# Attention logits from 64-row f32 products in two row halves, and the next pair's projection between the two transposes of a slot

## The chip, the cores and the metric

One NeuronCore of a Trainium2 chip runs the whole kernel. The metric is the time of one execution on the device in microseconds. The kernel before takes 1675.25 us, the median of 3 runs (1672.22 to 1677.1). The profiled execution took 1675.05 us, of which 1673.3 us are the span of the trace.

## What is computed

The input X is 32 sequences of 256 rows of 128 values, all f32. The output is X plus an attention plus a mixture of eight experts, both fed with the layer norm of X:

```python
x = L0_attn_X                       # (32, 256, 128)
xn = _layernorm(x)
x = x + attn(xn) + ffn(xn)

# attention: H = 16 heads of DQ = 64, NB = 10
Q, K, V = xn @ Wq + bq, xn @ Wk, xn @ Wv        # each (32, 16, 256, 64)
R = xn @ Wr + br                                 # (32, 16, 256, 10)
extra = einsum('bhtn,ntp->bhtp', R, D_ntT)       # bias by distance t - p, window of 128
logits = einsum('bhtd,bhpd->bhtp', Q, K) / 8 + bias + extra    # bias masks p > t and t - p >= 128
A = softmax(logits) @ V                          # (32, 256, 16 * 64)
return A @ Wproj + bproj

# ffn: of 8 experts (gelu, 512 wide) the two with the largest router logit
```

Rows 0 to 127 of a sequence see keys 0 to 127; rows 128 to 255 see all 256 keys. A head therefore has 3 x 128 columns of logits for 128 partitions.

## The kernel before, in words

Five engines run their own instruction lists and meet at semaphores: PE (TensorE), DVE (VectorE), ACT (ScalarE), POOL (GpSimd), and SP, which issues the DMAs. The kernel has four stages: a preparation up to about 150 us (loads, layer norm, router, weights), the attention of sequences 0 to 15, the experts (754 to 1004 us), and the attention of sequences 16 to 31. In each half POOL moves rows for the experts beside the attention, and in the second half DVE also adds the experts' rows to the output (`add_rows`, L1165, lines L1176).

Each half runs its first sequence, then a loop with two sequences in its body and seven turns, then its last sequence. The order of the work is written out by hand: `sequence` exists once for each engine and runs over 8 slots; slot j belongs to head pair j (heads 2j and 2j+1) of the sequence. There is no planner. An engine waits at a semaphore in the order in which its own code stands, so everything behind a waiting instruction waits too.

The logits of a pair are not computed from Q and K. Preparation makes one 128x128 matrix per head, `wm` (Wk of the head times Wq of the head, centred and scaled; L1278), split into an fp32r high part and an fp32r low part. `keys` (L1419) multiplies it with the transposed rows `xq`, also split, in three fp32r products for each head (`product`, L1331 to L1336). ACT rounds the result out of PSUM to `key_hi` (L810), and DVE subtracts that from the same PSUM bank to make `key_lo` (L1093). `logits` (L1437) then multiplies `xq` and the keys, again in three products: three of 256 columns for query rows 0 to 127 of both heads and three of 512 columns for rows 128 to 255.

One slot j of PE before:

1. `keys` of pair j+1 (6 products, 256 columns each)
2. `turn_probs` of head 2(j-3)+1: three 128x128 transposes (L1433)
3. `logits` of pair j (6 products)
4. the slot's unit at place 0
5. in even slots the values product of four heads (L1475; f32, 64 output columns in two column halves of the array, 8 products in 16 records), in odd slots the output product of four heads (L1487; 4 products in 8 records)
6. `turn_probs` of head 2(j-2)
7. the slot's unit at place 1

A unit is a piece of other work for this or the next sequence, always through one PSUM bank (`MISC_BANK`): "v" (V projection, 3 products of 512 columns), "r" (R projection, 6 products of 256 columns), or "g" (distance bias, one product of 512 columns, L1404). The table is UNITS at L358: 4 v, 2 r and 8 g per sequence.

DVE in slot j before: reciprocal of the sums of pair j-1 (L1121), copy of the transposed probabilities (`copy_probs`, L1111), `key_lo` of pair j+1, the four additions of logits and `extra` with their row minima (L1137, two of 128 columns, then two of 256), a second `copy_probs`, and copies of g units with tile 0 (L1088). ACT before: `key_hi` of pair j+1, its unit copies (v L784, r L790, g with tile 1 L795), the four exponentials of pair j (L826), and in even slots `headT` (L835). POOL scales the probabilities of pair j-1 (L687, L689), rounds the r unit of the slot before (L662) and issues the row moves.

PSUM has 8 banks. Before: keys 1, logits 3, transposes 1, values 1, units 1, outputs 1. The output product of a sequence accumulates over its four quads in one bank, and DVE adds it to `acc` once per sequence (L1160).

Of the kernel before, what the change touches and what calls it, by code (L numbers as in the profile page):

```python
# [5 lines left out]
ALU = mybir.AluOpType  # L6
# [7 lines left out]
P = 128  # L14
BANK = 512
# [33 lines left out]
def build(nc, X, Wq, bq, Wk, Wv, Wproj, bproj, Wr, br, b_nd, router_w, w1, b1, w2, b2, out):  # L49
# [24 lines left out]
    with ctx:  # L74
# [17 lines left out]
        wm_hi = sb("wm_hi", [P, H, P], F32R)  # L92
        wm_lo = sb("wm_lo", [P, H, P], F32R)
# [59 lines left out]
        wq_r = sb("wq_r", [P, H * DQ])  # L153
        wk_r = sb("wk_r", [P, H * DQ])

        top[0] = shared
        wqT = sb("wqT", [P, PAIRS, P])
        wkT = sb("wkT", [P, PAIRS, P])
# [14 lines left out]
        bq_r = sb("bq_r", [PAIRS, P])  # L173
        bqT = sb("bqT", [P, PAIRS])
        br_bc = sb("br_bc", [P, H * NB])
        qsum = sb("qsum", [P, PAIRS])
        ksum = sb("ksum", [P, PAIRS])
# [21 lines left out]
        key_hi = sb("key_hi", [P, 2, 2, T], F32R)  # L199
        key_lo = sb("key_lo", [P, 2, 2, T], F32R)  # L200
# [39 lines left out]
        def skew_rows(tile, head, count, first, size, pitch):  # L240
# [63 lines left out]
        key_high = sem("key_high")  # L304
        key_low = sem("key_low")
        s0_psum = sem("s0_psum")
        logit0_made = sem("logit0_made")
        s1_psum = sem("s1_psum")
        g_act = sem("g_act")
        g_dve = sem("g_dve")  # L310
        mean_psum = sem("mean_psum")
        centred = sem("centred")
        wq_centred = sem("wq_centred")
# [22 lines left out]
        PREP = [("w2", NX, False), ("small", 4, False), ("wq", 2, False), ("wk", 2, False),  # L336
                ("brev", 1, False), ("wm", 4, True), ("w1", NX, True)]
# [13 lines left out]
        H_BANK, Y_BANK, XB_BANK = (0, 1, 2, 3), (4, 5), (6, 7)  # L351
        KEY_BANK, S1_BANK, S0_BANK, PT_BANK, HEAD_BANK, MISC_BANK, OUT_BANK = 0, (1, 2), 3, 4, 5, 6, 7
        WR_MEAN_BANK, WV_MEAN_BANK = 5, (6, 7)
# [4 lines left out]
        UNITS = [(0, 0, "g", 2, 1, 0), (1, 0, "r", 0, 0, 1), (1, 1, "g", 3, 0, 0), (2, 0, "g", 3, 1, 0),  # L358
# [3 lines left out]
        UNITS_FINAL = [unit for unit in UNITS if not unit[5]]  # L362
        START = [("r", 0, 0), ("r", 1, 0), ("g", 0, 0), ("g", 0, 1), ("g", 1, 0), ("g", 1, 1), ("v", 0, 0), ("g", 2, 0)]
# [14 lines left out]
        def unit_taken(engine, kind, k, t, seq):  # L378
# [6 lines left out]
            elif t == 1:  # L385
                engine.wait_ge(g_act, 4 * seq + (k + 1))
            else:
                engine.wait_ge(g_dve, 4 * seq + (k + 1))
# [1162 lines left out]
```

## Time and profile before

| | value |
|---|---|
| median of 3 runs | 1675.25 us |
| profiled execution | 1675.05 us, span 1673.3 us |
| PE busy | 1510.8 us, 90% |
| PE weight loads busy | 1276.9 us, 76% |
| DVE busy | 1066.7 us, 64% |
| ACT busy | 988.9 us, 59% |
| POOL busy | 804.1 us, 48% |
| share of PE in the chain that ended last | 72% |

PE records overlap, because a product starts while the one before it drains; a duration of one record is longer than its distance to the next. How long PE takes for a piece of work is read from the start of its first record to the start of the next piece. A line of the timeline merges equal records and shows their count as x16, and the idle time before it, if any, in brackets with what ended it. A row of the windows view gives, for a stretch, its length and then the busy time of PE, weight loads, DVE, ACT and POOL, the granted clock of TensorE, and the DMA share.

### The profile page before, as it was taken

The numbers are of one execution on the slowest core, as the hardware profiler recorded it, in microseconds if no ns is written. First come the engines' busy times: TensorE is split into PE (matmuls) and PEld (weight loads), VectorE is DVE, ScalarE is ACT, GpSimd is POOL, SyncE is SP. The second block draws the span as 40 slices with busy tenths as digits, with TensorE's granted clock in tenths as the row PEclk, the third lists the DMA queues.
The fourth block names the chain that finished last, engine by engine and source line by source line (L and its number), as shares of the span: only waits on it lengthen the run. The fifth ranks groups of instructions, "written<-read, shape, count | busy, mean of one in ns | idle before, by whom it ended". The sixth has DMA issues, their size and how long they took to land.

```text
span 1673.3 us, 42585 instructions
## 1 busy us (share of the span) xinstructions
PE 1510.8 (90%) x10864; PEld 1276.9 (76%) x10864; DVE 1066.7 (64%) x3749; ACT 988.9 (59%) x2999; POOL 804.1 (48%) x1515
## 2 busy tenths in 40 slices
PE   2555999999999999989999997998989898989997
PEld 2224887878878887878999996787878787877885
DVE  5585777777767777762211112787868786877775
ACT  2223776766766676755554443676757675766664
POOL 0322766666666666650000001665656565656654
PEclk8686999999999999999999998999999999999999
DMA  9774555655555555655666664565555555656552
GB/s 285 271 274 120 163 168 145 177 166 165 155 160 168 152 159 145 180 154 160 201 202 205 206 202 136 155 174 135 167 143 161 150 149 143 166 142 180 145 158 70
DMA packets 375709, 282.62 MB, mean 169 GB/s; under 512 B 16626, under 2 KB 349988, under 8 KB 375588
## 3 DMA queue, kind: packets, MB, share of 16 engines
q1 hardware_dynamic: 367396, 264.64, 53.9%
q0 software_dynamic: 8192, 16.79, 3.5%
q14 instruction: 97, 0.79, 0.2%
q8 instruction: 24, 0.39, 0.1%
HBM read 168.05 MB, written 113.26 MB: 168 GB/s over the span
## 4 chain that ended last, share of the span: by engine, by line
PE 72%; DVE 9%; issue 8%; ACT 4%; SPq 3%; DMA 2%; DVEq 1%; POOL 1%; ACTq 0%; POOLq 0%
PE ps L1336 11%; PE ps L1334 11%; PE ps L1335 11%; PE ps L1475 10%; PE ps L1433 10%; PE ps L1370 8%; PE ps L1487 6%; PE ps L1404 3%; ACT prob L826 2%; DVE logit L1137 2%; DVE gst L1088 1%; DVE probT L1111 1%; DVE acc L1176 1%; SPq L453 1%; PE ps L1352 1%
## 5 line engine op out<-in xcount | busy, mean ns | idle before, releaser
L826 ACT ACTIVATE prob<-logit,low 128x128 f32<-128x128 f32 (+1 forms) x1024 | 454.2, 446 | 149.4 <-DVE low L1137 123.3
L1111 DVE COPY probT<-ps 128x384 f32<-128x384 f32 x512 | 284.5, 556 | 204.5 <-PE ps L1433 192.6
L687 POOL TENSOR_SCALAR prob<-prob,inv 128x128 f32<-128x128 f32 x512 | 188.6, 368 | 346.3 <-DVE inv L1121 336.7
L1137 DVE CUSTOM_DVE_ANT_0 logit<-ps,extra 128x128 f32<-128x128 f32 (+1 forms) x1024 | 303.3, 353 | 0.7 <-PE ps L1336 0.4
L1433 PE MATMUL ps<-ident,prob 128*128 128x128 f32 x1536 | 264.0, 281 | 12.1 <-DVE probT L1111 7.3
L1475 PE MATMUL ps<-probT,val 128*64 128x256 f32 (+1 forms) x2048 | 203.1, 342 | 44.1 <-DVE probT L1111 42.7
L689 POOL TENSOR_SCALAR prob<-prob,inv 128x256 f32<-128x256 f32 x512 | 241.4, 472 | 0.0
L1475 PEld LDWEIGHTS ps<-probT,val 128*64 128x64 f32 x2048 | 131.8, 141 | 130.7 <-issue 82.6
L1433 PEld LDWEIGHTS ps<-ident,prob 128*128 128x128 f32 x1536 | 175.0, 142 | 48.2 <-issue 40.7
L1334 PE MATMUL ps<-key_hi,xq_hi 128*128 128x256 f32 (+1 forms) x512 | 194.9, 381 | 0.0
L826 ACT ACTIVATION_READ_ACCUMULATOR prob<-logit,low 128x1 f32 x1024 | 192.9, 188 | 0.0
L662 POOL CAST r_hi<-r_raw 120x512 fp32r<-120x512 f32 x64 | 39.1, 610 | 301.7 <-ACT r_raw L790 301.7
L1093 DVE TENSOR_TENSOR key_lo<-ps,key_hi 128x512 fp32r<-128x512 f32 x256 | 175.3, 685 | 12.5 <-ACT key_hi L810 8.3
L1335 PE MATMUL ps<-key_lo,xq_hi 128*128 128x256 f32 (+1 forms) x512 | 175.2, 342 | 0.0
L1336 PE MATMUL ps<-key_hi,xq_lo 128*128 128x256 f32 (+1 forms) x512 | 174.0, 340 | 0.0
L810 ACT CAST key_hi<-ps 128x512 fp32r<-128x512 f32 x256 | 148.1, 579 | 34.3 <-PE ps L1336 34.3
L1334 PE MATMUL ps<-xq_hi,wm_hi 128*128 128x256 f32 x512 | 153.2, 299 | 4.5 <-DVE key_lo L1093 4.5
L672 POOL DMA_INDIRECT x_place<-xrow,at_now x128 | 131.9, 1031 | 39.9 <-issue 25.3
L1192 DVE TENSOR_TENSOR yrow<-ps,w2b 128x512 f32<-128x512 f32 x39 | 27.0, 692 | 189.7 <-PE ps L1370 189.7
L1370 PEld LDWEIGHTS ps<-w2b,hid 128*128 128x128 f32 x1248 | 145.2, 192 | 3.3
L674 POOL DMA_INDIRECT yget<-y_place,at_now x128 | 130.4, 1018 | 35.9 <-issue 24.3
L1335 PE MATMUL ps<-xq_lo,wm_hi 128*128 128x256 f32 x512 | 146.8, 287 | 0.0
(188 smaller groups left out, 3088.2 us busy)
## 6 DMA issues: line engine op xcount, KB each, us to landing
skew<-gst SPq DMA_DIRECT2D x256, 256.0 KB
extra<-skew SPq DMA_DIRECT2D x128, 512.0 KB, 3.9
extra<-skew SPq DMA_DIRECT2D x128, 256.0 KB, 3.6
w1b<-w_d SPq DMA_DIRECT2D x39, 514.0 KB, 3.5
w2b<-w_d SPq DMA_DIRECT2D x39, 320.0 KB, 3.3
x_place<-zero SPq DMA_DIRECT2D x39, 256.0 KB, 2.7
placed<-x_place SPq DMA_DIRECT2D x39, 256.0 KB, 3.7
y_place<-yrow SPq DMA_DIRECT2D x39, 256.0 KB, 2.2
```

What stands on the lines that cost most here:

```text
L687: nc.gpsimd.tensor_scalar(prob[:, h, 0:P], prob[:, h, 0:P], inv[:, h, 0:1], 1.0, ALU.mult, ALU.mult).then_inc(norm_made, 1)
L689: nc.gpsimd.tensor_scalar(prob[:, h, P:], prob[:, h, P:], inv[:, h, 1:2], 1.0, ALU.mult, ALU.mult).then_inc(norm_made, 1)
L826: ins = nc.scalar.activation(prob[:, h % PB, a:b], logit[:, h % LB, a:b], ACT.Exp, scale=-1.0, bias=low[:, h % LB, t:t + 1], accum_out=tot ...
L1093: nc.vector.tensor_tensor(key_lo[:, pair % 2, :, :].rearrange("p n k -> p (n k)"), ps[:, KEY_BANK, :], key_hi[:, pair % 2, :, :].rearrange ...
L1111: nc.vector.tensor_copy(probT[:, h % 4, :], ps[:, PT_BANK, 0:3 * P]).then_inc(pT_made, 1)
L1137: ins = nc.vector.tensor_tensor_reduce(out=logit[:, h % LB, a:b], in0=src, in1=extra[:, h, a:b], scale=1.0, scalar=BIG, op0=ALU.add, op1=A ...
L1334: nc.tensor.matmul(dst, a_hi, b_hi, start=start, stop=False)
L1335: nc.tensor.matmul(dst, a_hi, b_lo, start=False, stop=False)
L1336: return nc.tensor.matmul(dst, a_lo, b_hi, start=False, stop=stop)
L1370: mm = nc.tensor.matmul(ps[:, Y_BANK[u], t * P:(t + 1) * P], hid[:, u, c, t * P:(t + 1) * P], w2b[:, u, c * P:(c + 1) * P], start=(c == 0) ...
L1433: mm = nc.tensor.transpose(ps[:, PT_BANK, n * P:(n + 1) * P], prob[:, h % PB, n * P:(n + 1) * P], ident[:, :])
L1475: mm = nc.tensor.matmul(ps[DQ * n:DQ * n + DQ, HEAD_BANK, q], val[:, s, v:v + DQ], probT[:, hh % 4, p], start=(s == 0), stop=(s == 1), ski ...
```

## The change

`wm` is gone. The weights stay separate: `wqk`, centred Wq plus bias and centred Wk with the scale, each [128, 1024], split into high and low parts in preparation. `keys` of a pair now makes Q and K of both heads: for w in (Wq, Wk), three fp32r products of 256 columns. One ACT copy takes the bank to `qk`, in f32 and unsplit; DVE does nothing to it. `logits` of a pair is four f32 products with a contraction of 64: head 2j in rows 0 to 63 of the array, head 2j+1 in rows 64 to 127, each with its own PSUM bank. DVE's four additions wait for all of them.

The order in a slot changes on every engine. PE: logits of pair j; values or outputs; transposes of head 2(j-2); unit at place 0; keys of pair j+1; transposes of head 2(j-2)+1; unit at place 1. ACT: exponentials of pair j, then the unit copy (v or r), then the copy of pair j+1, then `headT`. DVE: reciprocal, four additions, `add_heads` in odd slots, both `copy_probs`, the g copy (all g copies are now DVE's), then the r correction of the same slot (L1102, before in the slot after). POOL rounds the r unit in its own slot too, ahead of the row moves.

The output product has no bank of its own any more. It goes into the bank of the values product, and DVE adds it to `acc` after each quad, four times per sequence instead of once.

```diff
-        UNITS = [(0, 0, "g", 2, 1, 0), (1, 0, "r", 0, 0, 1), (1, 1, "g", 3, 0, 0), (2, 0, "g", 3, 1, 0),
-                 (3, 0, "v", 0, 1, 0), (3, 1, "v", 1, 0, 0), (4, 0, "g", 0, 0, 1), (4, 1, "g", 0, 1, 1),
-                 (5, 0, "v", 1, 1, 0), (5, 1, "r", 1, 0, 1), (6, 0, "g", 1, 0, 1), (6, 1, "g", 1, 1, 1),
-                 (7, 0, "v", 0, 0, 1), (7, 1, "g", 2, 0, 1)]
+        UNITS = [(0, 0, "v", 0, 0, 0), (0, 1, "g", 3, 0, 0), (1, 0, "r", 0, 0, 1), (1, 1, "g", 3, 1, 0),
+                 (2, 0, "v", 0, 1, 0), (2, 1, "g", 0, 0, 1), (3, 0, "v", 1, 0, 0), (3, 1, "g", 0, 1, 1),
+                 (4, 0, "r", 1, 0, 1), (4, 1, "g", 1, 0, 1), (5, 0, "v", 1, 1, 0), (5, 1, "g", 1, 1, 1),
+                 (6, 1, "g", 2, 0, 1), (7, 1, "g", 2, 1, 1)]
...
 # PE
-                wait_from(pe, key_low, i * PAIRS + pair)
-                for n in range(2):
-                    h = 2 * pair + n
-                    mm = product(ps[:, KEY_BANK, n * T:n * T + T],
-                                 ((wm_hi[:, h, :], wm_lo[:, h, :]), (xq_hi[:, par, :], xq_lo[:, par, :])))
+                wait_from(pe, key_made, i * PAIRS + pair)
+                cols = slice(pair * P, (pair + 1) * P)
+                for w in range(2):
+                    mm = product(ps[:, KEY_BANK, w * T:(w + 1) * T],
+                                 ((wqk_hi[:, w, cols], wqk_lo[:, w, cols]), (xq_hi[:, par, :], xq_lo[:, par, :])))
...
+            def logits(i, pair):
+
+                pe.wait_ge(key_made, i * PAIRS + pair + 1)
                 wait_from(pe, logit_made, i * PAIRS + pair - 1)
-                product(ps[:, S1_BANK[pair % 2], :].rearrange("p (n k) -> p n k", n=2),
-                        ((xq_hi[:, par, P:T], xq_lo[:, par, P:T]),
-                         (key_hi[:, pair % 2, :, :], key_lo[:, pair % 2, :, :]))).then_inc(s1_psum, 1)
+                for q, k, cols in ((slice(0, P), slice(0, P), slice(0, P)), (slice(P, T), slice(0, T), slice(P, 3 * P))):
+                    for n in range(2):
+                        rows = slice(DQ * n, DQ * n + DQ)
+                        mm = nc.tensor.matmul(ps[:, S_BANK[pair % 2][n], cols], qk[rows, pair % 2, 0, q],
+                                              qk[rows, pair % 2, 1, k], start=True, stop=True)
+                mm.then_inc(s_psum, 1)
...
             def sequence(i, par, start, heads=True, more=True):
                 for j in range(PAIRS if heads else LAG):
+                    if heads:
+                        logits(i, j)
+                    if j % 2 == 0 and here(i, j - 4, heads, start):
+                        values(i, (j - 4) // 2)
+                    if j % 2 == 1 and here(i, j - 5, heads, start):
+                        outputs(i, (j - 5) // 2)
+                    if here(i, j - 2, heads, start):
+                        turn_probs(i, 2 * (j - 2))
+                    if heads:
+                        units(i, par, j, 0, more)
                     if heads and (j + 1 < PAIRS or more):
                         keys(i if j + 1 < PAIRS else i + 1, par if j + 1 < PAIRS else 1 - par, (j + 1) % PAIRS)
-                    if here(i, j - 3, heads, start):
-                        turn_probs(i, 2 * (j - 3) + 1)
...
                     if here(i, j - 2, heads, start):
-                        turn_probs(i, 2 * (j - 2))
+                        turn_probs(i, 2 * (j - 2) + 1)
                     if heads:
                         units(i, par, j, 1, more)
...
 # ACT, in sequence: the copy of the next pair behind the exponentials
-                    if heads and (j + 1 < PAIRS or more):
-                        keys(i if j + 1 < PAIRS else i + 1, (j + 1) % PAIRS)
-                    for n, kind, k, t, ahead in units_at(j, 0, more) if heads else []:
-                        unit(len(START) + i * len(UNITS) + n, kind, k, t, i + ahead)
...
                         ins.then_inc(prob_made, 1)
+                    for n, kind, k, t, ahead in units_at(j, 0, more) if heads else []:
+                        unit(len(START) + i * len(UNITS) + n, kind, k, t, i + ahead)
+                    if heads and (j + 1 < PAIRS or more):
+                        keys(i if j + 1 < PAIRS else i + 1, (j + 1) % PAIRS)
...
 # DVE
-                nc.vector.tensor_tensor(key_lo[:, pair % 2, :, :].rearrange("p n k -> p (n k)"), ps[:, KEY_BANK, :],
-                                        key_hi[:, pair % 2, :, :].rearrange("p n k -> p (n k)").bitcast(F32),
-                                        ALU.subtract).then_inc(key_low, 1)
...
+                        wait_apart(dve, s_psum, i * PAIRS + j + 1, const_made)
...
+            def add_heads(i, quad):
+                dve.wait_ge(out_psum, i * QUADS + (quad + 1))
+                wait_from(dve, attn_added, i * QUADS + quad)
+                seq = i if quad >= 0 else i - 1
+                x = acc[:, at(2 * seq, 2), :]
+                nc.vector.tensor_tensor(x, ps[:, HEAD_BANK, 0:2 * E].rearrange("p (t e) -> p t e", t=2), x,
+                                        ALU.add).then_inc(attn_added, 1)
...
 # preparation: transposes of Wq and Wk and the products to wm are gone; bq is loaded to all partitions
-            sp.dma_start(bq_r[:, :], bq.rearrange("(k d) -> k d", d=P)).then_inc(small_in, 16)
+            sp.dma_start(bq_bc[:, :], bq.partition_broadcast(P)).then_inc(small_in, 16)
```

## Rows read from the trace of the kernel before

**Rows 1.** Windows: one clean sequence, then the seven turns, of either half.

```profile
187.90:224.00 36.10, 35.95 (x275) 30.61 (x274) 27.81 (x104) 25.52 (x87) 24.23 (x47) 1.00 0.58 166
187.90:710.50 522.60, 507.81 (x3812) 431.65 (x3810) 389.67 (x1443) 360.99 (x1205) 338.58 (x643) 0.99 0.56 162
...
1111.70:1148.30 36.60, 36.13 (x275) 30.60 (x273) 29.75 (x112) 25.92 (x87) 24.15 (x47) 1.00 0.60 167
1075.00:1623.10 548.10, 516.16 (x3812) 436.37 (x3809) 416.13 (x1555) 364.04 (x1205) 337.57 (x643) 0.98 0.56 155
```

**Rows 2.** Timeline of PE: start us, length us, what (count).

```profile
504.62 0.48 PE L1334 MATMUL ps<-wv_hi,xq_hi 128*128 128x512 f32 x1
...
505.40 0.28 PE L1334 MATMUL ps<-xq_hi,wm_hi 128*128 128x256 f32 x1
...
505.99 0.28 PE L1336 MATMUL ps<-xq_hi,wm_lo 128*128 128x256 f32 x1
506.11 0.49 PE L1433 MATMUL ps<-ident,prob 128*128 128x128 f32 x3
506.35 0.37 PE L1334 MATMUL ps<-key_hi,xq_hi 128*128 128x256 f32 x1
...
507.48 0.39 PE L1404 MATMUL ps<-basis,rT 120*128 120x512 f32 x1
507.80 1.52 PE L1475 MATMUL ps<-probT,val 128*64 128x256 f32 x16
509.25 0.55 PE L1433 MATMUL ps<-ident,prob 128*128 128x128 f32 x3
509.64 0.50 PE L1404 MATMUL ps<-basis,rT 120*128 120x512 f32 x1
...
512.79 1.05 PE L1487 MATMUL ps<-wproj,headT 128*128 128x128 f32 x8
513.68 0.49 PE L1433 MATMUL ps<-ident,prob 128*128 128x128 f32 x3
```

**Rows 3.** Timeline of DVE, same columns, the bracket is idle time before.

```profile
507.79 0.28 DVE L1137 CUSTOM_DVE_ANT_0 logit<-ps,extra 128x128 f32<-128x128 f32 x1
...
508.90 0.69 DVE L1088 COPY gst<-ps 128x512 f32<-128x512 f32 x1
...
514.21 0.56 DVE L1111 COPY probT<-ps 128x384 f32<-128x384 f32 x1 [0.68 <-PE ps L1433]
...
519.65 0.74 DVE L1102 SCALAR_TENSOR_TENSOR rT<-r_hi,minus_low,r_raw 120x512 fp32r<-120x512 f32 x1
```

**Rows 4.** Groups by line, DVE, 1100 to 1640 us: count, busy us, mean ns.

```profile
L1176 DVE SCALAR_TENSOR_TENSOR acc<-yget,wtop,acc 128x128 f32 (+1 forms) x112 | 31.9, 347 | 0.0
```

**Rows 5.** Timeline of ACT, same columns.

```profile
508.41 0.40 ACT L826 ACTIVATE prob<-logit,low 128x128 f32<-128x128 f32 x1 [1.35 <-DVE low L1137]
...
510.18 0.56 ACT L835 COPY headT<-ps 128x512 f32<-128x512 f32 x1
...
515.24 0.57 ACT L790 COPY r_raw<-ps 120x512 f32<-120x512 f32 x1
515.70 0.58 ACT L810 CAST key_hi<-ps 128x512 fp32r<-128x512 f32 x1
```

**Rows 6.** Timeline around START: an ACT copy, and PE that waited for it.

```profile
145.75 0.58 ACT L795 COPY gst<-ps 128x512 f32<-128x512 f32 x1 [3.75 <-DMA skew<-gst]
...
146.38 0.79 PE L1334 MATMUL ps<-wv_hi,xq_hi 128*128 128x512 f32 x1 [1.83 <-ACT gst L795]
```

**Rows 7.** Timeline of DVE and PE at a turn of the loops.

```profile
487.33 0.18 DVE L1121 RECIPROCAL inv<-total 128x4 f32<-128x4 f32 x1 [2.81 <-issue]
...
488.33 2.83 PE L1475 MATMUL ps<-probT,val 128*64 128x256 f32 x16 [2.43 <-DVE probT L1111]
...
1311.60 0.18 DVE L1121 RECIPROCAL inv<-total 128x4 f32<-128x4 f32 x1 [4.12 <-issue]
```

**Rows 8.** The only 64-row product of the program, in preparation (length min/median/max).

```profile
L1278 PE MATMUL ps<-wqT,wkT x32: 272/272/419, 42.4 to 45.5; 64*128 64x128 f32 x32
```

More of the change, by code:

```diff
@@ L690, in sequence @@
                                                     ALU.mult, ALU.mult).then_inc(norm_made, 1)
-                    for n, kind, k, t, ahead in units_at(j - 1, 0, more) + units_at(j - 1, 1, more):
-                        if kind == "r" and heads:
+                    for n, kind, k, t, ahead in units_at(j, 0, more) if heads else []:
+                        if kind == "r":
                             round_weights(i + 1, k)
@@ L829, in sequence @@
                         ins.then_inc(prob_made, 1)
+                    for n, kind, k, t, ahead in units_at(j, 0, more) if heads else []:
+                        unit(len(START) + i * len(UNITS) + n, kind, k, t, i + ahead)
+                    if heads and (j + 1 < PAIRS or more):
+                        keys(i if j + 1 < PAIRS else i + 1, (j + 1) % PAIRS)
                     if j % 2 == 0 and here(i, j - 4, heads, start):
@@ L836, in sequence @@
                                        ps[:, HEAD_BANK, :]).then_inc(head_made, 1)
-                    for n, kind, k, t, ahead in units_at(j, 1, more) if heads else []:
-                        unit(len(START) + i * len(UNITS) + n, kind, k, t, i + ahead)
             def experts(b, u, k):
@@ L1121, in sequence @@
                         nc.vector.reciprocal(inv[:, h:h + 2, :], total[:, h:h + 2, :]).then_inc(inv_made, 1)
-                    if here(i, j - 3, heads, start):
-                        copy_probs(i, 2 * (j - 3) + 1)
-                    if heads and (j + 1 < PAIRS or more):
-                        keys(i if j + 1 < PAIRS else i + 1, (j + 1) % PAIRS)
                     if heads:
@@ L1207, in _ @@
                 for n, (kind, g, t) in enumerate(START):
-                    if kind == "g" and t == 0:
+                    if kind == "g":
                         positions(s0 * len(UNITS) + n, s0, g, t)
-                keys(s0, 0)
                 sequence(s0, s0)
@@ new lines, in values @@
+            def values(i, quad):
+                h = 4 * quad + 3
+                if quad == 0:
+                    pe.wait_ge(val_made, 4 * i + 2)
+                if quad == -2:
+                    pe.wait_ge(val_made, 4 * i)
+                pe.wait_ge(pT_made, i * H + h + 1)
+                wait_from(pe, attn_added, i * QUADS + quad)
+                for pair in range(2):
+                    for s in range(2):
+                        q = slice(pair * T, (pair + 1) * T) if s == 0 else slice(pair * T + P, (pair + 1) * T)
+                        p = slice(0, T) if s == 0 else slice(T, 3 * P)
+                        for n in range(2):
+                            hh = h - 3 + 2 * pair + n
+                            v = hh % H * DQ
+                            mm = nc.tensor.matmul(ps[DQ * n:DQ * n + DQ, HEAD_BANK, q],
+                                                  val[:, s, v:v + DQ], probT[:, hh % 4, p],
+                                                  start=(s == 0), stop=(s == 1), skip_group_check=True)
+                mm.then_inc(head_psum, 1)
@@ new lines, in outputs @@
+            def outputs(i, quad):
+                pe.wait_ge(head_made, i * QUADS + (quad + 1))
+                for t in range(2):
+                    for pair in range(2):
+                        mm = nc.tensor.matmul(ps[:, HEAD_BANK, t * E:(t + 1) * E],
+                                              headT[:, pair, t * P:(t + 1) * P],
+                                              wproj[:, (2 * quad + pair) % PAIRS, :],
+                                              start=(pair == 0), stop=(pair == 1))
+                mm.then_inc(out_psum, 1)
```

229 lines of the change are left out of this document (71 added, 158 removed).

## The prediction

> **What bounds the kernel now.** I read the windows first. In a clean sequence of the first half PE is busy 35.95 of 36.10 us, in the second half 36.13 of 36.60 us, at a granted clock of 1.00; DVE has 28 to 30 us and ACT 26 us of work in it [rows 1]. So PE sets the pace, and a slot is 4.5 us of PE work. Seven turns of the loop are fourteen sequences: 14 x 36.10 = 505.4 of 522.60 us, and 14 x 36.60 = 512.4 of 548.10 us [rows 1]. The rest, 17.2 and 35.7 us, together 52.9 us, falls on the six jumps back in each half: DVE stands idle there for 2.81 us (4.12 us in the second half) with nothing to wait for, and PE then waits for its `copy_probs` [rows 7].
>
> Next the timeline of PE, for the price of each piece, as the distance from its start to the next piece [rows 2]: v behind transposes 0.78; keys 0.71; three transposes 0.24, behind the values product 0.39; logits 1.13 (506.35 to 507.48); g 0.32 ahead of the values, where the array changes its tiling (a product of 512 columns without that is 0.23, so the change is 0.09); values 1.45; outputs 0.89.
>
> **The new logits on PE.** The values product is the nearest row: f32, pairs of products in the two column halves. 16 records are 8 pairs, four of 256 and four of 128 columns, in 1.45 us. The new logits are 8 records, two pairs of each kind: 0.73 us. With one change of tiling behind them, 0.82 us in place of 1.13. That takes the row halves to run side by side as the column halves do; the only 64-row product there is stands in one half at a time and does not tell [rows 8]. Bounds: 0.73, if the changes are in the 1.45 already; 1.54, if the halves do not overlap at all. In between: the weight loads of 128 columns might go one behind the other. Outputs have 8 such records in 0.89 us [rows 2], so that gives 0.98.
>
> The trace shows 0.09 us at a change of tiling, ahead of the values. The Trainium skill, TensorEngine Tiling (Array Packing), Key Properties, says that a change of tiling mode drains the array, while tiles of one mode load weights and multiply in parallel. The first half speaks against the change, with two more switches in every slot, 256 x 0.18 = 46 us by the row's price; the second half supports the 0.73.
>
> Keys keep their six products of 256 columns, transposes, values, outputs and the units keep their number. So PE's own work falls by 0.31 us per slot less the entry into the logits (0.09).
>
> **What ends last in a slot now: two chains.** Before, ACT and DVE had made the split keys of pair j+1 before they touched the logits of pair j. Now PE makes pair j+1 late in slot j, ACT copies it behind the exponentials of pair j, and the next thing PE does after T1 and one g is the logits that wait for it. Behind that wait stand all values, outputs and transposes. I count from the first record of logits j.
>
> Chain A, over PE. Even slot with a unit: logits 0.82, values 1.45, transposes 0.39, v (or r) 0.78, keys 0.71: issued by 4.15. The last record begins 0.12 before that and lasts 0.28 [rows 2]; the next engine starts 0.04 later (transposes end at 514.17, DVE starts at 514.21 [rows 2, 3]); the copy takes 0.58 [rows 5]; PE goes on 0.05 after an ACT copy (146.33 to 146.38 [rows 6]). Sum: 4.98. PE has only T1 and g to put beside it, 4.15 + 0.24 + 0.32 = 4.71: it waits 0.27. Slot 6, without v (and 0.08 for the step out of the transposes): 4.28. Odd slot: 0.82 + 0.89 + 0.24 + 0.78 + 0.71 = 3.44, so 4.27; slot 7: 3.57.
>
> Chain B, over DVE and ACT. The last pair of the logits begins at 0.51 and lasts 0.39, as a record of 512 columns does (an f32 product passes its 256 columns more than once) [rows 2]: 0.90. DVE starts 0.04 later, plus 0.12 for its second wait with a register (an estimate between 0 and 0.25, no row): 1.06. The exponentials begin 0.62 after the first addition (507.79 to 508.41 [rows 3, 5]) and take 1.77 (508.41 to 510.18 [rows 5]): 3.45. The unit copy 0.46 (515.24 to 515.70), the copy 0.58, PE 0.05: 4.54. In slots 6 and 7 no unit copy stands there: 4.08.
>
> Each slot takes the later: 0, 2 and 4 take 4.98 (A), 6 takes 4.28 (A), 1, 3 and 5 take 4.54 (B), 7 takes 4.08 (B). Sum 36.92.
>
> **DVE work that comes in the way.** It lost `key_lo` and got all g copies (0.69), four `add_heads` and, in slots 1 and 4, the r correction (0.74 [rows 3]) at the end of the same slot. In slot 4 the second transposes end at 4.64; `copy_probs`, g, r and the reciprocal, one behind the other, last until 6.5, and the additions of slot 5 were due at 4.98 + 1.06 = 6.04. So slot 5 is 0.48 longer. In slots 2 and 3 chain A covers the same or there is no r. Sum 37.40, against 36.10: +1.30 per sequence, x 16 = +21 us.
>
> In the second half `add_rows` adds four operations of 31.9/112 = 0.28 us, 1.14 us, at the end of slots 1 and 2 [rows 4]. Slot 1: g waits for the r copy (4.02), is out at 4.50; g copy, r, add_rows and reciprocal last until 7.02; due was 5.60. 1.42 late: slot 2 takes 4.54 + 1.42 = 5.96, 0.98 more than by A. Slot 2 ends in the same way 0.76 late, which slot 3 pays. 37.40 + 1.74 = 39.14, against 36.60: +2.54, x 16 = +41 us.
>
> **The jumps back.** DVE's last work in slot 7 is the g copy, which ends at 4.18. With the same pause of 2.81 us its additions start at 7.2 and not at 5.14: 2.05 late, slot 0 takes 6.59 for 4.98, +1.6. Second half, 1.31 more: +2.9. Six of each: 27 us against 52.9: -26 us. PE no longer waits for `copy_probs` there, and the slack of the other slots is gone anyway. DVE's list for the loop gets a few instructions shorter, so the pause might vanish (a rival below).
>
> The rows show DVE idle at the jump, released by nothing. The Trainium skill, Runtime: NRT & Kernel Launch, Instruction fetch mechanics, says that a taken branch to a target outside the small window of loaded instructions forces a fetch before the engine goes on; the trace agrees. Only a list that fits the window would be spared.
>
> **At nothing.** The output product's own bank: DVE's additions sit between slots and the next values follow 2 us later; without that cover 0.4 us per quad, 50 us. SP's writes and reads of the distance bias keep their number, and their g units come at least two slots ahead of the additions that need them. POOL's r rounding now waits for ACT in its own slot and holds up a row move of 1 us; POOL has 24 of 36 us of work [rows 1]. Preparation loses transposes and copies and gains a load of half a megabyte: between -3 and +3 us, I take 0. Experts: unchanged.
>
> **Sum.** +21 + 41 - 26 = +36 on the profiled execution's 1675.05 us, which is the median of the runs within 0.2 us: 1710 us in round numbers.
>
> **Rivals.**
>
> 1. *The chains are shorter than their sum, and PE sets the pace again.* For it: PE alone would need 33.4 + 8 x 0.09 = 34.2 us per sequence; every link was taken from rows where the engine was not hurried. Against it: the links stand in one line by the code, and each is a measured length. Full effect: 16 x (34.2 - 36.1) + 16 x (34.2 - 36.6) - 26 = -95, 1580 us. A chain shorter by 0.1 us per slot is 26 us; from 0.14 us per slot it decides for faster; at 0.27 (no wait in even slots) it is 1640 us. Chance 0.25.
> 2. *The halves load their weights one behind the other.* +0.16 us per slot, 256 slots, +41: 1751 us. Chance 0.12.
> 3. *The row halves do not overlap.* 1.54 for 0.82: +184: 1895 us. Chance 0.06. The pairs of the values product speak against it; nothing in the trace excludes it.
> 4. *DVE's loop fits now and the pause goes.* 27 us less: 1683 us, about no change. For it: fewer instructions in the body. Against: the body loses `key_lo` and one set of waits per slot but gets g copies and `add_heads`, a few per cent in all. Chance 0.07.
>
> My forecast has 0.50, with an own range of 1690 to 1735 (0.1 us per slot either way). Faster by over 0.3% (5 us, about what a measurement of this kernel can tell from none): most of rival 1 and a little of the forecast's edge, 0.27. Slower: forecast, 2, 3 and part of 4, 0.67. Between: 0.06. The range 1635 to 1775 leaves out rival 3, the full form of rival 1 and little else.
>
> **What would show it.** PE idle in every slot just ahead of the logits, released by the ACT copy, 0.2 to 0.3 us in even and 0.5 in odd slots; a busy PE of about 33 us in a sequence of 37.4 and 39.1 us; logits records in pairs, 0.73 us from first record to the next piece; longer slots 5, and 2 and 3 in the second half, with DVE still at r or `add_rows` when the logits are there. Sequences under 36 us would make it wrong in sign. Records of the logits one after another would be rivals 2 or 3. Equal sequences before and after with shorter jumps would be rival 4 or a part of 1.

## The result, and the profile after

The changed kernel takes 1731.24 us, the median of 4 runs (1727.19 to 1740.91), beside 1675.99 us of the kernel before on the same chip: ratio 1.034, 95% interval 1.030 to 1.039. It is slower by 55 us. The forecast was 1710 us, 35 us slower.

The page of the profile first, the lines that say most:

```profile
span 1730.2 us, 43010 instructions
PE 1533.4 (89%) x11335; PEld 1185.5 (69%) x11335; DVE 1024.0 (59%) x3715; ACT 924.8 (53%) x2864; POOL 807.1 (47%) x1515
PE 59%; ACT 14%; issue 10%; DVE 9%; SPq 4%; DVEq 1%; DMA 1%; POOL 1%; ACTq 0%; POOLq 0%
L1351 PE MATMUL ps<-basis,rT 120*128 120x512 f32 x256 | 129.4, 506 | 56.6 <-ACT val L757 36.3
L1391 PEld LDWEIGHTS ps<-qk 64*128 64x128 f32 x2048 | 137.3, 190 | 88.7 <-ACT qk L776 69.9
```

The third line is the chain that ended last: ScalarE has come into it. The last two lines show what PE now waits for: the unit copy (`val`) ahead of a g product, and the copy of the projection (`qk`) ahead of the logits, where the wait is booked on the weight load. Both copies stand behind the exponentials on ScalarE.

The windows of the changed kernel answer to [rows 1]: a clean sequence, then the seven turns, of the first and of the second half (window, its length, then busy us of PE, PE's weight loads, DVE, ACT and POOL, granted clock, DMA share, GB/s).

```profile
464.36:502.08 37.72, 36.35 (x288) 27.84 (x289) 26.21 (x103) 23.97 (x82) 24.49 (x47) 1.00 0.56 163
190.51:738.99 548.48, 518.72 (x4033) 396.48 (x4033) 368.38 (x1429) 335.35 (x1148) 340.69 (x644) 0.98 0.54 155
1391.57:1431.20 39.63, 37.15 (x289) 27.86 (x289) 28.42 (x111) 23.97 (x82) 24.24 (x47) 1.00 0.54 152
1102.33:1678.84 576.51, 528.09 (x4032) 395.45 (x4033) 397.37 (x1541) 335.46 (x1148) 338.87 (x644) 0.99 0.53 147
```

Against [rows 1] the turns take 25.9 and 28.4 us more, 54.3 of the 56.9 us by which the span grew. Clean sequences: 14 x (37.72 - 36.10) + 14 x (39.63 - 36.60) = +65.1 us. Turns less 14 clean sequences: 20.4 + 21.7 = 42.1 us, where it was 52.9: -10.8 us. The first logits start at 152.4 us, where they started at 153.6, so preparation, put at nothing, is 1.2 us shorter.

Distances between the starts of successive logits, slots 0 to 7, from the trace (clean sequences):

```
forecast, half 1       4.98 4.54 4.98 4.54 4.98 5.02 4.28 4.08   37.40
after, half 1          4.93 4.56 4.94 4.56 4.96 4.97 4.28 4.51   37.71
forecast, half 2       4.98 4.54 5.96 5.30 4.98 5.02 4.28 4.08   39.14
after, half 2          4.95 4.56 5.92 5.37 4.96 5.14 4.28 4.46   39.64
```

One odd slot (slot 1) of the changed kernel, in the timeline of PE, DVE and ACT, answers to [rows 2, 3, 5]:

```profile
469.29 0.93 PE L1391 MATMUL ps<-qk 64*128 64x128 f32 x8
470.15 1.16 PE L1421 MATMUL ps<-wproj,headT 128*128 128x128 f32 x8
...
470.36 0.29 DVE L1093 CUSTOM_DVE_ANT_0 logit<-ps,extra 128x128 f32<-128x128 f32 x1
...
470.99 0.40 ACT L788 ACTIVATE prob<-logit,low 128x128 f32<-128x128 f32 x1 [1.26 <-DVE low L1093]
...
472.76 0.56 ACT L763 COPY r_raw<-ps 120x512 f32<-120x512 f32 x1
472.90 0.49 PE L1380 MATMUL ps<-ident,prob 128*128 128x128 f32 x3
473.22 0.58 ACT L776 COPY qk<-ps 128x512 f32<-128x512 f32 x1
...
473.38 0.49 PE L1351 MATMUL ps<-basis,rT 120*128 120x512 f32 x1
473.85 0.93 PE L1391 MATMUL ps<-qk 64*128 64x128 f32 x8
```

That is the forecast's chain B link by link: additions 1.07 after the logits' start (1.06 forecast), exponentials 0.63 later (0.62), 1.77 for them, 0.46 for the unit copy, 0.63 for the copy and the step to PE. The logits take 0.86 (469.29 to 470.15; 0.82 forecast).

### The profile page after: what moved, and what is told of

Same layout as the page of the kernel before. It is cut to its first block, busy times and chain, and to the rows that moved or that the text cites. A ratio compares the mean times of both kernels' runs of the same rounds, so it can differ in the third digit from the quotient of the medians.

```text
span 1730.2 us, 43010 instructions
## 1 busy us (share of the span) xinstructions
PE 1533.4 (89%) x11335; PEld 1185.5 (69%) x11335; DVE 1024.0 (59%) x3715; ACT 924.8 (53%) x2864; POOL 807.1 (47%) x1515
## 4 chain that ended last, share of the span: by engine, by line
PE 59%; ACT 14%; issue 10%; DVE 9%; SPq 4%; DVEq 1%; DMA 1%; POOL 1%; ACTq 0%; POOLq 0%
PE ps L1391 11%; ACT prob L788 9%; PE ps L1316 8%; PE ps L1411 8%; PE ps L1380 6%; PE ps L1280 5%; PE ps L1282 5%; PE ps L1281 5%; PE ps L1351 4%; PE ps L1421 4%; DVE logit L1093 2%; ACT val L757 2%; ACT qk L776 2%; DVE acc L1135 1%; DVE rT L1064 1%
## 5 line engine op out<-in xcount | busy, mean ns | idle before, releaser
L1391 PE MATMUL ps<-qk 64*128 64x128 f32 (+1 forms) x2048 | 243.0, 356 | 14.5 <-ACT qk L776 8.0
L1057 DVE COPY gst<-ps 128x512 f32<-128x512 f32 x256 | 175.7, 686 | 58.3 <-PE ps L1351 48.4
L1391 PEld LDWEIGHTS ps<-qk 64*128 64x128 f32 x2048 | 137.3, 190 | 88.7 <-ACT qk L776 69.9
L1411 PE MATMUL ps<-probT,val 128*64 128x256 f32 (+1 forms) x2048 | 194.7, 332 | 2.7 <-issue 1.4
L1411 PEld LDWEIGHTS ps<-probT,val 128*64 128x64 f32 x2048 | 127.1, 136 | 81.5 <-issue 43.0
L1351 PE MATMUL ps<-basis,rT 120*128 120x512 f32 x256 | 129.4, 506 | 56.6 <-ACT val L757 36.3
L776 ACT COPY qk<-ps 128x512 f32<-128x512 f32 x256 | 148.3, 579 | 37.0 <-PE ps L1282 30.2
L1421 PEld LDWEIGHTS ps<-wproj,headT 128*128 128x128 f32 x1024 | 129.4, 198 | 44.9 <-issue 43.1
L1421 PE MATMUL ps<-wproj,headT 128*128 128x128 f32 x1024 | 154.2, 296 | 1.4 <-ACT headT L801 1.4
L1280 PE MATMUL ps<-xq_hi,wqk_hi 128*128 128x256 f32 x512 | 151.4, 296 | 0.0
```

The source lines that it names most:

```text
L1280: nc.tensor.matmul(dst, a_hi, b_hi, start=start, stop=False)
L1351: mm = nc.tensor.matmul(ps[:, MISC_BANK, :], rT[:, n // 2, a:a + P], basis[:, :], start=True, stop=True)
L1391: mm = nc.tensor.matmul(ps[:, S_BANK[pair % 2][n], cols], qk[rows, pair % 2, 0, q], qk[rows, pair % 2, 1, k], start=True, stop=True)
L1411: mm = nc.tensor.matmul(ps[DQ * n:DQ * n + DQ, HEAD_BANK, q], val[:, s, v:v + DQ], probT[:, hh % 4, p], start=(s == 0), stop=(s == 1), ski ...
L1421: mm = nc.tensor.matmul(ps[:, HEAD_BANK, t * E:(t + 1) * E], headT[:, pair, t * P:(t + 1) * P], wproj[:, (2 * quad + pair) % PAIRS, :], st ...
```

## The experiments

All times are medians with the ratio to the kernel before, measured beside it on the same chip. "After" stands at 1.034.

| run | us | ratio (interval) |
|---|---|---|
| old order, 64-row logits | 1629.1 | 0.974 (0.971 to 0.977) |
| projection right behind the logits | 1823.9 | 1.090 (1.087 to 1.094) |
| after, DVE loops written out | 1673.2 | 1.001 (0.999 to 1.002) |
| logits head by head | 1729.1 | 1.034 (1.031 to 1.037) |
| one more exponential on ACT | 1811.3 | 1.082 (1.080 to 1.084) |
| projection of Q twice on PE | 1769.8 | 1.056 (1.054 to 1.058) |
| both heads in one row half | 1850.6 | 1.105 (1.102 to 1.107) |
| old order, DVE loops written out | 1608.5 | 0.960 (0.959 to 0.962) |
| before, DVE loops written out | 1620.0 | 0.969 (0.966 to 0.972) |
| projection alone put back | 1830.7 | 1.094 (1.091 to 1.098) |
| old order, transposes together | 1839.8 | 1.101 (1.098 to 1.104) |
| old order, projection of Q twice | 1699.3 | 1.017 (1.013 to 1.021) |

**The arithmetic with the old order.** PE, ACT and DVE get the order of before. The products stay those of the change, and so do the new table of units, DVE's copies of g and the bank that values and outputs share.

```diff
 PE, slot j:
+    keys(j + 1)
+    turn_probs(i, 2 * (j - 3) + 1)
     logits(i, j)
+    units(place 0)
     values or outputs
     turn_probs(i, 2 * (j - 2))
-    units(place 0)
-    keys(j + 1)
-    turn_probs(i, 2 * (j - 2) + 1)
     units(place 1)
 ACT, slot j:
+    keys(j + 1); units(place 0)
     exponentials(j)
-    units(place 0); keys(j + 1)
 DVE: copy_probs(2(j-3)+1) to the slot's head, r correction one slot later
```

> The changed kernel's arithmetic (64-row float32 logits, both projections), with the order of the kernel before on PE, ACT and DVE: projection of the next pair at the slot's head, its copy ahead of the exps, one transpose at the head and one at the end, r correction and second probability copy a slot later. Theory (the copy of the projection behind the exps makes the two chains): both chains are gone, PE sets the pace with 34.2 us a sequence worked out from its pieces against 37.7 and 39.7 measured in the changed kernel, so about 1731 - 16 x 3.5 - 16 x 5 = 1595, up to 1625 if half 2 keeps its add_rows waits. Rival (the new logits themselves, or PE's own work, make it slow, and the order is innocent): 1700 or more.

Measured 1629.1 us, 43 us faster than before and 102 us faster than after. That is 4 us above the top of the expected range, but the chain theory held and the rival fell. The order costs 1.034 - 0.974 = 6.05%, 101 us. All the rest of the change gains 2.6%, 44 us: the new arithmetic, together with the table of units and the shared bank, which no run separates from it. The windows (clean sequences of the two halves) show PE busy throughout:

```profile
446.75:482.22 35.47, 35.47 (x290) 27.85 (x289) 26.75 (x103) 23.80 (x83) 24.24 (x47) 1.00 0.59 169
1321.04:1356.69 35.65, 35.65 (x290) 27.90 (x289) 28.50 (x111) 23.73 (x83) 24.46 (x47) 1.00 0.63 175
```

35.5 us, not the 34.2 that I had taken from PE's pieces. An even slot is 4.95 with nothing waited for. The transposes ahead of the logits take 0.42 to 0.48 to the logits' start, where three transposes took 0.24:

```profile
460.58 0.49 PE L1381 MATMUL ps<-ident,prob 128*128 128x128 f32 x3
461.00 0.93 PE L1392 MATMUL ps<-qk 64*128 64x128 f32 x8
```

Behind the logits, v up to the values takes 0.90 where v up to the projection takes 0.78, but 0.08 of that is the step into the values, which the forecast had priced; its first product takes 0.34 behind the logits and 0.32 behind transposes. Outputs right behind the logits take 0.99 for 0.89 (470.15 to 471.14 in the changed kernel).

**One more operation on ScalarE, one more on PE.** The two chains predict different prices for added work.

```diff
+ nc.scalar.activation(spare[...], logit[head 2j+1, long part], ACT.Exp, ..., accum_out=spare[...])
```

> The changed kernel with one more ScalarE instruction pair in each slot, behind the four exps: the last long exponential once more, into a spare tile (0.49 us with its accumulator read in the changed kernel's trace). Nothing waits for it but what stands behind it on ScalarE, the copies. Theory (the copy behind the exps is in the chain of every slot): slots 1, 3, 5 and 7 take the whole 0.49, slots 0, 2, 4 and 6, where the copy starts 0.05 to 0.15 after ScalarE was free, 0.35 to 0.45: 3.4 to 3.7 us a sequence, 1731 + 108 to 120 = 1839 to 1851. Rival (PE sets the pace, ScalarE is 53% busy): 1731.

Measured +80 us, below the 108 to 120 expected. Slots 1, 3 and 5 take the whole of it (4.56 to 5.05 in slots 1 and 3), slots 0, 2, 6 and 7 take 0.2 to 0.4, slot 4 only 0.1: a sequence grows by 2.8, not by 3.5, and the jumps give another 12 us back. Every slot grows by added ScalarE work, but I had overrated by how much in the even ones. An engine busy 53% of the span decides here; the rival that PE sets the pace would have seen nothing. The waits of PE between 190 and 640 us (what PE waited for, us in total, times, longest), first after, then this run:

```profile
PE ps L1351 <- ACT val L757: 7.6, 16, 0.8
```

```profile
PE ps L1355 <- ACT val L758: 24.2, 42, 1.2
```

```diff
-                for w in range(2):
+                for w in (0, 0, 1):
                     mm = product(ps[:, KEY_BANK, ...
```

> The changed kernel with the Q half of each pair's projection computed twice (three more products of 256 columns, 0.355 us on PE in each of 256 slots, same result). Theory (two chains, PE's lateness binds slots 0, 2, 4 and 6 alone; in slots 1, 3 and 7 the projection ends about 0.6 us before ScalarE is free to copy it): 0.3 to 0.36 in four slots of eight, nothing in the others: 1731 + 38 to 46 = 1769 to 1777, and the odd slots stay at 4.56 and 4.4. Rival (PE sets the pace): 0.355 in each slot, 1731 + 91 = 1822. Rival (only ScalarE's chain): 1731.

Measured 1769.8 us, inside the expectation, though not in each slot as expected: slots 0, 2, 4 and 6 took 0.32 to 0.37, slots 1 and 3 rose from 4.56 to 4.80, and slot 7 fell to 4.24. My 0.6 of slack in odd slots was too much: in slot 1 after, the projection's last record ends at 473.06 and its copy starts at 473.22. The lines of such a slot in this run show why it took 4.80:

```profile
487.36 0.48 PE L1351 MATMUL ps<-basis,rT 120*128 120x512 f32 x1
487.96 0.93 PE L1391 MATMUL ps<-qk 64*128 64x128 f32 x8
```

PE still waits here, 0.60 from g's start to the logits for 0.32 of work, now for the copy of a late projection. That is chain A. Without the added 0.36 it is 4.44 long in an odd slot (the forecast had 4.27), only 0.12 under chain B. So the two chains stand close together in odd slots, and a third of the added PE work was covered. PE's own work is below both.

The same PE edit in the kernel with the old order:

> The kernel with the order of before and 64-row logits (1629 us), with the Q half of each projection computed twice, as in the run that cost the changed kernel 39 us. Theory (with this order PE sets the pace in every slot): 0.355 in each of 256 slots, 1629 + 91 = 1720, between 1710 and 1722. Rival (waits for VectorE or ScalarE set part of the slots here too): 1665 to 1690.

Measured 1699.3, +70 us. Slots 1 to 4 and 6 grew by 0.35 or 0.36 (4.95 to 5.31, 4.25 to 4.61), slot 7 by 0.32, slots 0 and 5 by 0.29 and 0.25: PE sets the pace there, but for some 0.1 us of slack in slots 0 and 5. A clean sequence grew by 2.64 and 2.47 us, 82 us in 32 of them; 12 us come back at the jumps, whose extra time fell from 30.5 to 18.8 us. I had let the jumps stay as they were, and so was 20 us too high.

**The row halves.** Only the order of the four products changes:

```diff
-  for q, k, cols in (short, long):
-      for n in range(2):
+  for n in range(2):
+      for q, k, cols in (short, long):
```

> The changed kernel with the four products of a pair's logits issued head by head (head 0 short and long, then head 1 short and long) instead of the two heads alternating. Theory (products in the two row halves overlap only with a neighbour in the other half): now only the long one of head 0 meets the short one of head 1, so logits take about 1.2 us instead of 0.86, 0.3 to 0.4 more in each of 256 slots: 1731 + 75 to 100 = 1805 to 1830. Rival (no overlap in either order): 1731 unchanged. Rival (the two run beside each other in any order): 1731 too, with logits at 0.86.

Measured: no change, 1729.1 us; logits 0.86. (Beneath the unchanged total a clean sequence was 0.26 and 0.43 us shorter in the two halves, in slot 7 and in slot 5 of the second half; the turns cost 6 us more beyond their clean sequences, with the clock at its lower level after 10 of the 12 jumps.)

```profile
495.69 0.93 PE L1391 MATMUL ps<-qk 64*128 64x128 f32 x8
496.55 1.16 PE L1421 MATMUL ps<-wproj,headT 128*128 128x128 f32 x8
```

My theory (overlap only between neighbours in the program) fell. The next run tells the two rivals apart:

```diff
-  rows = slice(DQ * n, DQ * n + DQ)
+  rows = slice(0, DQ)
```

> The changed kernel with both heads of a pair read from rows 0 to 63 of the projections (the second head's logits are then the first's, so this is not the reference's result): the four products of the logits all stand in one row half. Theory (the 0.86 us of the logits is two row halves at work together): the four now run one behind the other, 1.4 to 1.5 us, 0.55 to 0.65 more in each slot, and logits are in every chain: 1731 + 140 to 165 = 1871 to 1896. Rival (the halves never overlapped, the products are just cheap): 1731, logits 0.86.

```profile
492.13 1.57 PE L1391 MATMUL ps<-qk 64*128 64x128 f32 x8
493.64 1.16 PE L1421 MATMUL ps<-wproj,headT 128*128 128x128 f32 x8
```

1.51 us against 0.86 for the same eight records, and 1850.6 us (+119). So the halves do run at the same time, and two halves at once are what makes the new logits cheap. The size of the whole was 20 us under my range, as a clean sequence of half 1 grew by 4.4 us and not by 8 x 0.65 = 5.2: part of the added time fell into waits that were there anyway.

**The projection's place.** Two versions move it alone. In the first, PE takes it right behind the logits:

> The changed kernel with one move on PE alone: the projection of the next pair right behind the logits; ACT and DVE keep their order. Theory (chain A, PE late with the projection, holds slots 0, 2, 4 and 6; chain B, the copy behind the exps, holds the rest and stays): even slots 4.6 to 4.8 instead of 4.95, slot 6 about 4.1, odd slots unchanged at 4.56; 0.7 to 0.9 us a sequence, so 1731 - 22 to 29 = 1702 to 1709. Rival (only PE's own lateness matters): 1620 or less. Rival (the place of the projection doesn't matter): 1731.

Measured 1823.9 us: +93 where I expected 22 to 29 less. All my cases fell. An even slot of it, timeline of PE and ACT:

```profile
493.71 0.93 PE L1391 MATMUL ps<-qk 64*128 64x128 f32 x8
494.57 0.39 PE L1280 MATMUL ps<-xq_hi,wqk_hi 128*128 128x256 f32 x1
...
497.78 0.40 PE L1282 MATMUL ps<-wv_hi,xq_lo 128*128 128x512 f32 x1
498.22 0.59 ACT L757 COPY val<-ps 128x512 f32<-128x512 f32 x1 [0.78 <-PE ps L1282]
498.30 0.52 PE L1380 MATMUL ps<-ident,prob 128*128 128x128 f32 x3
498.70 0.59 ACT L776 COPY qk<-ps 128x512 f32<-128x512 f32 x1
...
499.34 0.93 PE L1391 MATMUL ps<-qk 64*128 64x128 f32 x8
```

The projection is out 3.2 us ahead of its copy, but ScalarE copies the unit first, and v is 0.7 us later on PE now. ScalarE stands idle for 0.78 us, then makes both copies, and the logits wait: 5.63 us instead of 4.93. "PE late with the projection" was the wrong name for chain A; it is "PE late with the last product whose copy stands ahead of the logits". The odd slots, which I had expected unchanged, went from 4.56 to 4.98 in the same way: in slot 1 ScalarE stands idle for 0.33 us ahead of the copy of r. In slot 6, which has no v, nothing but the second transposes stood behind the first, and they wait for DVE's copy: 5.19 for 4.28.

In the second, the projection and its copy go back to the slot's head:

> The changed kernel with the projection alone put back: on PE at the slot's head, its copy on ScalarE ahead of the exps; the unit of the slot stays behind the first transpose on PE and behind the exps on ScalarE, and both transposes stay in one slot. Theory (PE is held wherever something behind the exps on ScalarE is needed before the slot ends; now it is the unit's copy that the next basis product waits for): a slot with a unit is logits to end of exps 3.5 (even) or 3.9 (odd), copy 0.5 and signal 0.1, basis product 0.3 to 0.4, projection 0.7: 5.1 to 5.2 even, 5.5 to 5.6 odd, slots 6 and 7 about 4.0; 39.5 to 40 a sequence instead of 37.7, so 1731 + 55 to 75 = 1786 to 1806, slower than the changed kernel. Rival (the projection's place is what made it slow): 1629 to 1660.

1830.7 us: slower than after, as the theory said and the rival did not, and by 25 us more than its range. Slots with a unit missed in opposite directions (even 5.38, 5.1 to 5.2 expected; odd 5.23, 5.5 to 5.6 expected); slots 6 and 7 took 5.0 and 4.6 to 4.9 where I had 4.0. In those two nothing lies between the transposes any more. The last version shows the price of that by itself:

```diff
 (old order)
-    turn_probs(i, 2 * (j - 3) + 1)        at the slot's head
     ...
     turn_probs(i, 2 * (j - 2))
+    turn_probs(i, 2 * (j - 2) + 1)
```

> The kernel with the order of before and 64-row logits (1629 us), but with the two transposes of a pair directly one behind the other at the slot's end, on PE and in VectorE's copies. Theory (the second transpose needs the bank that VectorE empties, 0.56 for the copy and 0.1 to 0.2 of signals, and nothing of PE lies between them): 0.45 to 0.75 of waiting in each slot, so 3.6 to 6 us a sequence and 1629 + 110 to 190 = 1740 to 1820. Rival (the waits fall into time that PE has to spare): 1629 to 1650.

1839.8 us, +211 us, more than the range. PE's waits between 190 and 640 us, and the transposes of one slot:

```profile
PE ps L1380 <- DVE probT L1073: 55.2, 65, 1.1
...
500.73 0.55 PE L1380 MATMUL ps<-ident,prob 128*128 128x128 f32 x3
502.11 0.52 PE L1380 MATMUL ps<-ident,prob 128*128 128x128 f32 x3 [0.83 <-DVE probT L1073]
```

The second transposes start 1.38 us after the first, where PE needs 0.3 to 0.4 for them. Copy and signals are 0.83 of that; the rest is the 0.55 that the first transposes last to their end, which I had left out.

This is what the projection does in its new place: with v or r it fills the time in which DVE empties the transposes' one bank. The place covers one wait and opens another.

**The jumps back.**

```diff
-                with dve.Fori(0, HALF // 2 - 1) as m:
+                for m in range(HALF // 2 - 1):
```

> The changed kernel with VectorE's two attention loops written out in line, all other engines still looping. Theory (the 41 us that the 12 jumps back cost over clean sequences are VectorE's pause at its own jump): no pause, about 1731 - 41 = 1690, between 1685 and 1700. Rival (the time at a jump is PE's or ACT's own, or straight code is fetched no faster and the stall only spreads out): 1725 to 1745.

```profile
450.69:487.80 37.11, 36.23 (x288) 27.81 (x289) 26.02 (x103) 23.87 (x82) 24.34 (x47) 1.00 0.56 164
190.92:710.40 519.48, 507.62 (x4033) 389.74 (x4033) 364.33 (x1429) 334.44 (x1148) 340.64 (x645) 1.00 0.57 163
1347.67:1386.62 38.95, 36.85 (x288) 27.88 (x289) 28.18 (x111) 23.84 (x82) 24.22 (x47) 1.00 0.55 155
1074.95:1621.62 546.67, 516.64 (x4032) 390.18 (x4032) 394.21 (x1541) 333.99 (x1148) 339.35 (x645) 1.00 0.55 155
```

1673.2 us, 58 less than after and more than the 41 expected. Turns less 14 clean sequences: -0.1 and +1.4 us; of the 42 us at the jumps 41 are gone. Some 18 us more are in the clean sequences, 0.61 and 0.68 less each: odd slots 4.47 for 4.56, slot 7 4.08 for 4.5. In the loop DVE's waits compare a semaphore with a register; written out, they compare with constants. In slots 1 and 3 DVE's first addition then starts 0.97 us after the logits instead of 1.07, which fits the 0.12 that the forecast had estimated for a register. In slot 7 more passes between the reciprocal and the first addition, with nothing named to wait for (the bracket). The timeline of DVE at slot 7, first after, then with the logits head by head:

```profile
498.52 0.17 DVE L1083 RECIPROCAL inv<-total 128x4 f32<-128x4 f32 x1
498.99 0.29 DVE L1093 CUSTOM_DVE_ANT_0 logit<-ps,extra 128x128 f32<-128x128 f32 x1 [0.30 <-issue]
```

```profile
496.63 0.17 DVE L1083 RECIPROCAL inv<-total 128x4 f32<-128x4 f32 x1
496.78 0.29 DVE L1093 CUSTOM_DVE_ANT_0 logit<-ps,extra 128x128 f32<-128x128 f32 x1
```

The second kernel has the same instructions on DVE, register waits included, and no idle time at this place; its slot 7 is 4.18. So the register alone does not explain slot 7, and what does is not shown.

The same edit in the two other kernels:

> The kernel before, with VectorE's two attention loops written out in line and nothing else changed. Theory (52.9 us of the kernel before is VectorE's pause at its own 12 jumps back, and a slot that PE sets gains nothing else): 1675 - 53 = 1622, up to 1632 if the written-out stream costs 8 us as it did in the kernel with the old order and 64-row logits. Rival (the pause is mostly other engines' own): 1650 or more.

1620.0 us, as forecast: the kernel before can have the larger part of the best kernel's gain by this edit alone.

> The kernel with the order of before and 64-row logits (1629 us), and VectorE's two attention loops written out in line. Theory (its 12 jumps back cost 1.5 to 3.6 us each over a clean sequence, 28 us in all, and VectorE's pause at its own jump is the cause): 1629 - 28 = 1601, between 1597 and 1606; the slots themselves don't change, since PE and not VectorE sets them here. Rival (a straight stream of instructions costs as much in fetches): 1620 to 1630.

1608.5 us, 2 us above the range. The 30.5 us at the jumps went down to 1.2, but a clean sequence grew by 0.12 and 0.55 us: slot 7 went from 3.60 to 3.93, and to 4.13 in half 2. In slot 7 of the first half DVE's first `copy_probs` starts 0.93 after the logits instead of 0.10, its additions start 1.40 after them instead of 1.07, and the next transposes wait for the copy behind these. What holds the first copy is not shown. This is the best kernel of the study, 0.960 of the kernel before. Against the written-out kernel before (0.969) the new arithmetic, with table and bank, still gains, but 0.9% and no longer 2.6%.

## Why the prediction came out as it did

- **The new logits, 0.82 for 1.13.** 0.86 measured, from the pairs of the values product. Rival 2 (weight loads in a row, 0.98) has at most a quarter of its 0.16, rival 3 is out: only in one row half do the records take 1.51, close to the 1.54 of the bound.
- **Chains A and B.** Right in every slot from 0 to 6 within 0.07 us, apart from slot 5 of half 2 (+0.12). PE's wait ahead of the logits was there in even slots (0.59 from g's start to the logits, 0.32 of it work), but the mark I named for it, PE busy 33 us in a sequence, was wrong: 36.35, since modelled ends count the pipeline's tail as busy. In odd slots the larger part of the wait stood ahead of g, for the unit's copy (0.24; 472.90 to 473.38 for 0.24 of work), and 0.15 ahead of the logits.
- **Slot 7, 4.08.** 4.35 to 4.5. DVE's additions start 1.3 to 1.4 after the logits, where the chain had 1.06. Written out, they start at 1.03 and the slot is 4.08; head by head, 1.09 and 4.18. A dearer register wait, for which I had 0.12 without a row, can be a part of it; the cause is open. This and the second half's slots make +65 us in the loops, where the forecast's 14 x 1.30 + 14 x 2.54 gives 54.
- **DVE's late work.** Slot 5 (4.97 for 5.02) and `add_rows` in slots 2 and 3 (5.92 and 5.37 for 5.96 and 5.30) are confirmed. With the old order the same `add_rows` cost 0.2 us a sequence instead of 1.9.
- **The jumps, the step that failed in size.** Forecast 27 us, measured 42, so -11 instead of -26. Slot 0 behind the jump: 12 slots of 7.0 to 7.6 for 4.94, together 27.5 us more, the 27 of the sum. That this agrees is luck, since two errors cancel: I had 10 and 17 us for the two halves, and it is 14 in each. DVE's last g copy ends 0.77 after the logits of slot 0 and not 0.10, because in slot 7 the second transposes wait 0.5 us for the copy of the first, a wait that I had put at nothing. And the longer pause of the second half did not come. DVE's idle time at the jump, one turn of each half:

```profile
424.53 0.18 DVE L1083 RECIPROCAL inv<-total 128x4 f32<-128x4 f32 x1 [2.49 <-issue]
...
1349.62 0.18 DVE L1083 RECIPROCAL inv<-total 128x4 f32<-128x4 f32 x1 [2.17 <-issue]
```

  It is 2.2 to 2.5 us in all 12 turns, where it was 2.3 to 2.8 in the first half and 4.1 to 4.6 in the second half of the kernel before; why is not shown. The rest of the 42 is nearly all slot 1, 6.0 to 7.3 for 4.56 in 7 of the 12 turns, 13 us. I had ended the account when DVE was back. But PE, held by DVE and ACT, had done little for 4 us, and its clock fell. Windows of after from the jump at 421 us, the turn with the longest stretch at the lower level:

```profile
421.30:424.90 3.60, 3.60 (x33) 2.68 (x34) 0.91 (x3) 0.00 (x0) 1.41 (x4) 1.00 0.65 181
424.90:428.90 4.00, 1.88 (x11) 1.03 (x10) 2.23 (x10) 3.19 (x11) 1.60 (x4) 0.91 0.74 212
428.90:432.00 3.10, 3.10 (x16) 2.45 (x16) 1.97 (x10) 0.79 (x4) 1.62 (x4) 0.50 0.28 87
432.00:436.20 4.20, 4.08 (x24) 3.77 (x23) 1.32 (x3) 2.35 (x8) 0.61 (x1) 0.64 0.00 0
436.20:441.10 4.90, 4.90 (x40) 3.59 (x40) 3.50 (x14) 2.83 (x11) 2.37 (x6) 1.00 0.47 125
```

  PE is busy 1.88 of 4.00 us, then the granted clock is 0.50 (the lower level, 1.2 GHz), and the eight logits records take 1.59 instead of 0.86:

```profile
428.89 1.65 PE L1391 MATMUL ps<-qk 64*128 64x128 f32 x8
430.48 2.07 PE L1421 MATMUL ps<-wproj,headT 128*128 128x128 f32 x8
```

  In the seven turns with a long slot 1 the clock fell, in the other five it stayed and slot 1 took 4.56. PE had been about as busy there (1.96 of 4.00 us in the turn at 343 us, at a granted clock of 1.00), so what decides between them is not shown. The trace of the kernel before already held this cost. Its clock fell at 8 of the 12 jumps, and in the first half slot 0 took 8.1 to 8.5 us there and 6.6 to 6.8 at the other jumps. Windows of before, from the jump at 409 us:

```profile
408.73:412.70 3.97, 1.77 (x12) 1.21 (x12) 1.37 (x4) 1.35 (x4) 1.85 (x5) 1.00 0.82 232
412.70:416.80 4.10, 4.10 (x27) 3.34 (x24) 1.87 (x11) 2.33 (x10) 0.93 (x3) 0.58 0.74 210
```

  So the 52.9 us were not DVE's pause alone, though all of it hangs on the jump (written out, the kernel before took 1620.0 us), and the forecast took the clock's part of them away without putting one back. The pause itself did not vanish, so rival 4 is out. The cause is the jump of DVE, shown by writing the loop out; that it is the fetch of instructions, as the Trainium skill says in Runtime: NRT & Kernel Launch, Instruction fetch mechanics, agrees with that and was not tested by itself.
- **Rival 1, PE sets the pace.** It failed for this order and holds for the old one, where a clean sequence is 35.5 us: the 34.2 of its price was 1.3 us too low, mostly the dearer neighbours of the logits. By 35.5 instead of 34.2 its full effect would have been some 40 us smaller.

## What to carry to other kernels

A cheaper operation gains only if the order keeps what it needs off the end of another engine's queue: here the new products, with table and bank, gained 44 us and their order lost 101. Before moving a step, list on each engine's queue what stands ahead of its copy and what stands behind its wait, and follow that around one whole slot; moving the projection by itself made it 93 and 99 us worse. When a stall is priced, go on until TensorE's clock is back, and look at the granted clock of the stall in the trace that is at hand.

## What was not expected of the hardware

- Products in the two row halves overlapped although the program had two products of one half in a row: with head 0 short, head 0 long, head 1 short, head 1 long, the eight records still took 0.86 us, as in the alternating order. Two halves 0.86, one half 1.51 us.
- A 64-row product made its full-height neighbours dearer: transposes to logits 0.42 us where three transposes take 0.24, outputs behind logits 0.99 for 0.89. The Trainium skill, TensorEngine Tiling (Array Packing), Key Properties, has a drain at each change of tiling mode; that the steps at such a change are longer here agrees with it.
- DVE stood idle for 2.2 to 2.5 us at each jump back of the changed kernel (up to 4.6 in the kernel before). Written out, the same work ran without any such pause at those places, in three kernels (58, 50 and 21 us gained in all).
- A stall at a jump lowered TensorE's clock at 7 of 12 jumps of the changed kernel and at 8 of 12 of the kernel before. In the changed kernel slot 1 took 1.5 or 2.7 us more where it fell.
